# Two layers on one core: reordered scan output, scan-input work moved off GpSimd, attention squares, residual add and prologue moved

## The reference, cut to what matters

```
L0 attention:  h_tan = arcsinh(|h|)/|h| * h ;  q,k,v = h_tan @ w*.T        (16 heads of 16)
               q_hyp, k_hyp = sinh(|.|)/|.| * (.) ;  times = sqrt(1/c + |.|^2)
               probs = softmax(-(q_hyp.k_hyp - q_time*k_time)/4) ;  out = probs @ v @ wo.T
L0 ffn:        fp4 quantised gate/up/down, silu(gate)*up
L1 scan:       x_in, z = split(x @ in_w.T) ;  u = silu(conv4(x_in)) ;  dt, B, C from u
               dt = clip(softplus(dt_raw*w + b), 1e-4, 10)
               h_t = h_{t-1}*exp(dt_t*A) + dt_t*B_t*u_t ;  y_t = h_t.C_t       (512 channels x 16 states)
               out = (layernorm(y)*g + b + D*u) * silu(z) @ out_w.T
L1 ffn:        token-shift mix, sigmoid(r) * (relu(k)^2 @ W_v)
```

## Time and profile before

| phase | us from the start | span, us |
|---|---|---|
| attention | 0 to 2957 | 2957 |
| first ffn | 2957 to 3645 | 688 |
| scan input | 3645 to 4335 | 690 |
| scan | 4335 to 5715 | 1380 |
| scan output | 5715 to 6122 | 407 |
| last ffn | 6122 to 6371 | 249 |
| span of the profiled execution | | 6371.1 |
| profiled execution, device time | | 6372.78 |
| median of three runs | | 6380.58 |

### The profile page before, as it was taken

How to read it: one execution, slowest core, us unless ns; L and a number is a source line. 1 busy time by engine, 2 the same in 40 slices (tenths; PEclk the granted TensorE clock), 3 DMA queues, 4 the chain that set the end, 5 groups by cost and what they waited for, 6 DMA issues and landing times. The chain is left out here.

```text
span 6371.1 us, 94620 instructions
## 1 busy us (share of the span) xinstructions
PE 5160.2 (81%) x27420; PEld 2063.8 (32%) x27420; DVE 4908.5 (77%) x10471; ACT 3773.4 (59%) x5329; POOL 1359.8 (21%) x1658
## 2 busy tenths in 40 slices
PE   6979889797979979796999854426888888877878
PEld 3333333333333333332566522211111111115555
DVE  6666575766667576665888688888999999987768
ACT  4555555555555555553444366666888888874434
POOL 0000000000000000000111134454444444434411
PEclk8989989898989989797999976665555555559999
DMA  0000000000000000000111123332111111124422
GB/s 24 1 14 1 14 1 1 14 1 14 1 14 1 1 14 1 8 1 27 35 41 43 49 88 117 120 117 73 50 49 50 49 50 49 51 68 149 150 91 73
DMA packets 198904, 273.56 MB, mean 43 GB/s; under 512 B 13989, under 2 KB 157989, under 8 KB 192454
## 3 DMA queue, kind: packets, MB, share of 16 engines
q1 hardware_dynamic: 181190, 252.90, 13.0%
q10 hardware_dynamic: 17408, 16.78, 0.8%
HBM read 151.14 MB, written 118.49 MB: 42 GB/s over the span
## 5 line engine op out<-in xcount | busy, mean ns | idle before, releaser
L644 DVE TENSOR_REDUCE at_nmax<-at_ps_t 128x1 f32<-128x512 f32 x2048 | 1320.8, 686 | 583.2 <-PE at_ps_t L344 565.8
L486 ACT ACTIVATE at_probsT<-at_ps_s 128x1024 f32<-128x1024 f32 x1024 | 1045.9, 1023 | 808.8 <-PE at_ps_s L369 808.8
L2044 DVE SCALAR_TENSOR_TENSOR sc_decayed<-sc_da,sc_state 128x256 f32<-128x256 f32 x2048 | 775.5, 424 | 9.3 <-ACT sc_da L1999 8.2
L2054 DVE CUSTOM_DVE_ANT_0 sc_state<-sc_xd,sc_decayed 128x256 f32<-128x256 f32 x2048 | 755.6, 408 | 0.0
L2006 ACT ACTIVATE sc_xd<-sc_ps_du,sc_bt 128x512 f32<-128x512 f32 x1024 | 649.9, 692 | 176.8 <-PE sc_ps_du L1947 176.8
L344 PE MATMUL at_ps_t<-at_qkT 108*128 108x512 bf16 x2048 | 711.0, 412 | 42.9 <-DVE at_nmax L644 19.5
L1912 POOL TENSOR_SCALAR sc_xd<-sc_xd 128x1024 f32<-128x1024 f32 x512 | 532.2, 1039 | 804.9 <-ACT sc_xd L2006 804.9
L1936 PE MATMUL sc_da<-sc_parts,sc_sel 24*128 24x512 bf16 x1024 | 566.0, 609 | 118.5 <-DMA sc_sel<-sc_sel 81.6
L1947 PE MATMUL sc_ps_du<-sc_parts,sc_sel 24*128 24x512 bf16 x1024 | 565.2, 609 | 112.5 <-ACT sc_xd L2006 112.5
L378 PE MATMUL at_ps_o<-at_probsT,at_v 128*32 128x256 f32 x8192 | 632.7, 392 | 1.2
L365 PE MATMUL at_ps_s<-at_qkT 108*128 108x512 bf16 x2048 | 623.6, 387 | 0.0
(11 more groups left out here) (308 smaller groups left out, 7990.8 us busy)
## 6 DMA issues: line engine op xcount, KB each, us to landing
dt_parts<-si_pt SPq DMA_DIRECT2D x64, 384.0 KB, 2.6
du_parts<-si_pu SPq DMA_DIRECT2D x64, 384.0 KB, 3.2
sc_parts<-dt_parts SPq DMA_DIRECT2D x128, 192.0 KB
sc_parts<-du_parts SPq DMA_DIRECT2D x128, 192.0 KB
u_tok<-si_ut SPq DMA_DIRECT2D x8, 2048.0 KB, 8.3
y<-sc_yo SPq DMA_DIRECT2D x256, 64.0 KB
so_yin<-y SPq DMA_DIRECT2D x32, 512.0 KB
so_uin<-u_tok SPq DMA_DIRECT2D x32, 512.0 KB
```

The costliest lines, as they stand in the source:

```text
L486: nc.scalar.activation(probsT[:, c % RING, :], ps_s[c % 2][:], ACT.Exp).then_inc(s_exp, 1)
L644: nc.vector.tensor_reduce(nmax[:, par, c, t:t + 1], ps_t[c][:], AX_X, ALU.max, negate=True).then_inc(s_max, 1)
L2044: nc.vector.scalar_tensor_tensor(decayed[:, ch], da[q % 2][:, j % 2, ch], DECAY_MIN, state[:, (j - 1) % SRING, ch], ALU.max, ALU.mult).the ...
L2054: nc.vector._custom_dve(bass.dve_ops.TENSOR_ADD_SAT, out=state[:, j % SRING, ch], in0=xd[:, q % RING, j % 2, ch], in1=decayed[:, ch], s0=S ...
```

## The change

In attention: `LEAD` 14 to 12; `joined` from tile 2 to 4, `row_turned` and `rows_stored` from tile 5 to 6; POOL's hbo behind the splits of heads 0 and 1; in `finish`, ACT's squares two at a time behind the first four attT copies and the roots behind the fifth, DVE's series behind its fourth residual add and the log arguments behind the seventh.

In scan input: 1+exp on ACT (`raised`), the remainders on DVE (`rests`), POOL left with one memset; the tile buffers four deep; ACT's split in two halves (`first_parts` of tile t, `second_parts` of t-1), DVE's third parts of t-2; the convolution writes u directly instead of acc.

In scan output: the turning of the gated result is put first in PE's step and the gT copies first in ACT's; the store of p-3 and the x root of p-2 stand in step p, `x_norm` is done for p-2; xsum, xout and x statistics get two buffers; SP's loads no longer wait for x_sums (only the residual's load does); the first two steps are written out ahead of the loop.

```diff
-    LEAD = 14
+    LEAD = 12
             def splits(b):
                 split(b, 0, 0)
                 split(b, 1, 1)
+                nc.gpsimd.tensor_tensor(hbo[:], hb[:], bo_bc[:]...broadcast_to([P, TB, D]), ALU.add).then_inc(s_hbo, 1)
...
             def finish(b, more):                                     # ACT
-                if more:
-                    squares(b + 1)
-                    log_roots(b + 1)
                 for t in range(TB):
                     ...
                     nc.scalar.copy(attT[:, u]...)
+                    if more and t < QUAD:
+                        square(2 * t)
+                        square(2 * t + 1)
+                    if more and t == QUAD:
+                        log_roots(b + 1)
...
         def _(pool):                                                 # scan input
             nc.gpsimd.memset(xc[:, :, 0:PAD], 0.0).then_inc(s_zero, 1)
-            with pool.Fori(0, B) as b:
-                for t in range(TB):
-                    nc.gpsimd.tensor_tensor(ex1[:, t], ex[:, t], one_col..., ALU.add).then_inc(s_ex1, 1)
-                for t in range(TB):
-                    nc.gpsimd.tensor_tensor(dt[:, w], dt[:, w], pt[:, w, 0], ALU.subtract).then_inc(s_tr, 1)
-                    nc.gpsimd.tensor_tensor(du[:, w], du[:, w], pu[:, w, 0], ALU.subtract).then_inc(s_ur, 1)
+            def raised(t):                                           # ACT
+                nc.scalar.activation(ex1[:, t], ex[:, t], ACT.Copy, bias=1.0).then_inc(s_ex1, 1)
                 for t in range(TB):                                  # ACT
-                    split(b - 1, t)
+                    first_parts(b - 1, t)
+                    if t >= 1:
+                        second_parts(b - 1, t - 1)
-                for t in range(1, TB):                               # DVE
-                    products(b, t)
-                    third_parts(b, t - 1)
+                for t in range(1, TB + 2):
+                    if t < TB:
+                        products(b, t)
+                    if t <= TB:
+                        rests(b, t - 1)
+                    if t >= 2:
+                        third_parts(b, t - 2)
...
             def step(p, w):                                          # scan output, SP
-                sp.wait_ge(s_sum, p - 2)
                 sp.wait_ge(s_turned, 2 * p - 2)
                 sp.wait_ge(s_cent, 2 * p - 2)
                 sp.wait_ge(s_skip, 2 * p - 2)
                 load(p, w)
+                    sp.wait_ge(s_sum, p - 2)
                 load_residual(p - 1, 1 - w)
             def step(p, w):                                          # PE
+                gated_turned(p - 1, 1 - w)
                 z_products(p)
                 x_turned(p + 1, 1 - w)
-                out_products(p - 1, 1 - w)
+                out_products(p - 1)
             def step(p, w):                                          # ACT
+                outs(p - 1)
                 gates(p, w)
                 xT_stored(p + 1)
-                outs(p - 1)
-                x_root(p - 1)
+                    store(p - 3, 1 - w)
                 y_root(p + 1)
-                store(p - 1)
+                    x_root(p - 2, w)
             def step(p, w):                                          # DVE
                 x_sums(p - 1, 1 - w)
-                x_norm(p - 1)
+                    x_norm(p - 2, w)
```

More of the change, by code:

```diff
@@ L404, in head @@
                         outputs(b, hd, c - 2)
-                    if c == 5 and left:
+                    if c == 6 and left:
                         row_turned(b, hd + 1, 1 - par)
@@ L671, in head @@
                         row_max(b, hd + ahead, (par + ahead) % 2, t)
-                    if c == 2 and left:
+                    if c == 4 and left:
                         joined(b, hd + 1, 1 - par)
@@ L893, in finish @@
                     nc.vector.tensor_tensor(hbo[:, t], ps_o[t % 2][:, 0:D], hbo[:, t], ALU.add).then_inc(s_y, 1)
+                    if more and t == QUAD - 1:
+                        log_series(b + 1)
+                    if more and t == QUAD + 2:
+                        log_arguments(b + 1)
                 dve.wait_ge(s_y, b * TB + TB)
@@ L1448, in ssm_input_phase @@
         s_stu = sem("u_saved")
[L1449 to L1450 removed]
+        s_stt = [sem(f"dt_parts_saved{w}") for w in range(RING)]
+        s_std = [sem(f"du_parts_saved{w}") for w in range(RING)]
         x_v = x2.rearrange("b (n p) d -> p b n d", p=P)
@@ L1668, in _ @@
             for t in range(TB):
-                split(B - 1, t)
+                first_parts(B - 1, t)
+                if t >= 1:
+                    second_parts(B - 1, t - 1)
+            second_parts(B - 1, TB - 1)
         @block.vector
@@ L2128, in ssm_output_phase @@
         s_x3 = sem("x3_ready")
-        s_st = sem("x3_saved")
+        s_st = [sem(f"x3_saved{w}") for w in range(2)]
         tiles = lambda a: a.rearrange("b (n p) d -> p (b n) d", p=P)
@@ L2137, in schedule @@
             first()
-            with eng.Fori(0, PAIRS // 2 - 1) as it:
+            step(1, 1)
+            step(2, 0)
+            with eng.Fori(1, PAIRS // 2 - 1) as it:
                 step(2 * it + 1, 1)
@@ L2164, in step @@
                 load(p, w)
+                if not (isinstance(p, int) and p == 2):
+                    sp.wait_ge(s_sum, p - 2)
                 load_residual(p - 1, 1 - w)
@@ L2169, in _ @@
             load_residual(0, 0)
-            with sp.Fori(0, PAIRS // 2 - 1) as it:
+            step(2, 0)
+            step(3, 1)
+            with sp.Fori(1, PAIRS // 2 - 1) as it:
                 step(2 * it + 2, 0)
@@ L2221, in z_products @@
             def z_products(p):
-                pe.wait_ge(s_zs, 2 * p)
+                if not (isinstance(p, int) and p == 0):
+                    pe.wait_ge(s_zs, 2 * p)
                 for u in range(2):
@@ L2236, in out_products @@
                     last.then_inc(s_gt, 1)
-                pe.wait_ge(s_sum, p)
+            def out_products(p):
+                if not (isinstance(p, int) and p == 0):
+                    pe.wait_ge(s_sum, p)
                 for u in range(2):
@@ L2343, in x_sums @@
                     dve.wait_ge(s_o, 2 * p + u + 1)
-                    last = nc.vector.tensor_tensor(xsum[:, u], ps_o[u][:, 0:D], xres[:, w, u], ALU.add)
+                    last = nc.vector.tensor_tensor(xsum[:, w, u], ps_o[u][:, 0:D], xres[:, w, u], ALU.add)
                 last.then_inc(s_sum, 1)
@@ L2362, in y_gated @@
                 dve.drain()
-                if not (isinstance(p, int) and p == 0):
+                if not (isinstance(p, int) and p < 2):
                     dve.wait_ge(s_gt, 2 * p - 2)
@@ L2393, in step @@
                 x_sums(p - 1, 1 - w)
-                x_norm(p - 1)
+                if not (isinstance(p, int) and p < 2):
+                    x_norm(p - 2, w)
             def last_steps():
                 y_gated(PAIRS - 1, 1)
-                for p, w in ((PAIRS - 2, 0), (PAIRS - 1, 1)):
-                    x_sums(p, w)
-                    x_norm(p)
+                x_sums(PAIRS - 2, 0)
+                x_norm(PAIRS - 3, 1)
+                x_norm(PAIRS - 2, 0)
+                x_sums(PAIRS - 1, 1)
+                x_norm(PAIRS - 1, 1)
             schedule(dve, first, step, last_steps)
```

144 lines of the change are left out of this document (79 added, 65 removed).

## The result

The changed kernel takes 6226.41 us, the median of four runs (6223.75 to 6227.39), against 6379.23 us for the kernel before (6377.47 to 6382.16): a ratio of 0.976, 95% interval 0.974 to 0.978. That is 153 us less. The forecast was 6223. Part of so close a hit is luck: 157 us were forecast, and from one profiled execution to the other (6372.78 and 6226.35 us) 146 were gained; the rest of the 153 is that the profiled execution of the kernel before ran 6 us under its median.

The account below looks back on a forecast made before the run. No engine was full in the three phases: waits bound scan output, and POOL slowed DVE in scan input and at one attention copy. 53 + 46 + 58 = 157 us off 6380.6 gave 6223 us, range 6200 to 6250.

Parts of the forecast that it names:

- the loads were no limit: Scan output, rival (a): loads set the pace at 12 us a pair, gain 12 us instead of 58, 6269 us; chance 0.12.
- the ring of rival (d): Scan output: PE's turning, DVE's product, ACT's silu and z wait on each other, 18.5 us a pair, 6490 us; chance 0.02.
- the 0.2 us for the skip term: Scan output: allowance per pair for POOL's skip term sharing something with DVE, raising DVE's step from 9.7 to 9.9 us.
- convolution: Scan input: DVE's convolution of a batch, with POOL idle and a 0.9 us late token start, falls from 24.4 to 20.2 us.
- wait: Scan input: new DVE wait at the first remainder for ACT's first cast, 2.7 us a batch, lost in full.
- tile: Scan input: a token tile on DVE becomes eight instructions of 0.60 us and one of 0.34, 5.14 us.
- The 1 us a turn kept for the edges: Scan input: 1 us a loop turn deducted for effects of four-deep buffers and the longer ACT queue at the edges.
- advice that the forecast set against the change: Scan input: move work off saturated DVE to Scalar or GpSimd; by it alone the phase sum would be 67 us worse.
- Projection and packing: Attention: DVE's copy no longer blocked by POOL's residual add, 4.3 us in each batch but the first, 30 us.
- Heads: Attention: two tiles moved from the prologue are made up in the main loop on PE, costing 0.9 us a batch.
- Finish: Attention: first attT copy starts 2.6 us sooner, net 1.1 us a batch, 8 us in all, bounds -5 to 18.
- the 1.5 us a batch set aside for squares and roots between the copies: Attention finish: deductions of 0.5 us for squares and about 1.0 us for roots with a table load.

Follow-up runs that it names:

- parts_a: Kernel after with POOL's residual add back in front of the heads, 1+exp back on POOL, scan output's loads behind the sums again; 6260.6 us.
- parts_c: Kernel after with squares and roots before attT copies, DVE's series before its residual adds, remainders one tile later, no bias in skip term (output lacks it); 6186.3 us.
- warm_late: Kernel after with 24 idle identity transposes on PE in front of its wait for DVE at a batch's start in scan input; 6214.1 us.
- parts_b: Kernel after with a prologue of 14 tiles, the two remainders back on POOL, scan output's root, norm and store one pair back; 6283.4 us.
- two: Kernel after with scan output's normalising moved from DVE to ACT and scan input's remainders one tile later; 6191.6 us.

## Why the prediction was right

**What bounds the phases.** In scan output the reading of who sets the pace held: PE's wait for gT went, DVE became the pace, the loads were no limit (parts_a), the ring of rival (d) stayed open (PE waits 1.7 us for the product, and DVE for nothing). Of the sizes, 48 us in each phase against 58, 46 and 53, those of scan input were met term by term, and that of attention is a sum of misses that partly cancel.

**Scan output, 58 against 48.** The term that was mis-sized is the 0.2 us for the skip term. With one of POOL's two operations gone a pair is 0.86 us shorter (9.46 against 10.32, parts_c). The forecast said that the adds "move to another place in the step"; it did not look where. They begin when DVE's product ends, and last some 5.7 us; DVE's next 4 us are statistics and a PSUM add, which ran at their length, and the normalising behind them is caught by the fourth. In the kernel before it mostly was not (453 ns in the mean, 809 now). That is 2 x 0.36 = 0.7 us a pair, 22 us in all; without it a pair would be 9.6 us, close to the 9.7 that the forecast worked out for DVE without contention.

**Scan input, 46 against 48.** Each term was met: convolution 20.3 (20.2 forecast), wait 2.37 (2.7), tile 5.15 (3913.03 to 3918.18; 5.14 forecast). The 1 us a turn kept for the edges was 1.1, but that it fits is luck: its cause was not the buffers or the queue, it is TensorE's clock at the start of a batch (warm_late). The 16 instructions added to DVE cost nothing net, since each had been paid for in slowed neighbours: parts_b gives the same work back to POOL and loses 27 us. What the forecast did not see is that its two moves do not add up: with the remainders on DVE the move of 1+exp brought nothing (parts_a), with them on POOL the kernel before and parts_b differ by 21 us (687.6 and 666.6; parts_b also has the deeper buffers and the split in halves). The Trainium skill's rule on the two sides of SBUF (SBUF — State Buffer, SBUF: two separate sides), that a DVE operation with two SBUF inputs and a GpSimd operation that reads SBUF exclude each other, agrees with these rows. The Trainium skill's advice that the forecast set against the change (Perfetto Trace Analysis, Optimizing Scalar/DVE Operations) goes on to say that moving work between GpSimd and DVE might not help, since they share a read port; the forecast left that out. Here such a move off DVE cost 27 us.

**Attention, 53 against 48.** The parts, from the starts of projection, prologue, first logits and last output of all batches, are these. Projection and packing fell from 81.0 us to 76.8 in batches 1, 3, 5 and 7, by 4.2 us where 4.3 was forecast, but to 78.3 to 78.6 in 2, 4 and 6: 24 us and not 30. Prologue 20.2 to 17.5, 8 x 2.7 = 22 us, as forecast. Heads +1.2 us a batch, 0.9 forecast, but batch 0's +7.0. Finish 19.6 to 17.0, 18 us where 8 was forecast: the 1.5 us a batch set aside for squares and roots between the copies did not show. So 48 came near 53 by misses both ways: the forecast had 14 us too much in the projections and the heads, and 10 too little in the finish.

The two shortfalls, in the projections and in batch 0's heads, are one thing. In batch 2 the eighth projection ran at half clock, in batch 3 it did not, with the same wait in front of it:

```profile
769.15 4.34 PE L434 MATMUL at_ps_s<-at_wqkvT,at_hT 128*128 128x512 f32 x8 [2.23 <-ACT at_hT L581]
```
```profile
1129.91 2.85 PE L434 MATMUL at_ps_s<-at_wqkvT,at_hT 128*128 128x512 f32 x8 [2.24 <-ACT at_hT L581]
```

And batch 0's first 22 us of heads ran at 0.50, in parts_c, whose instructions there are the same, at 0.81. In the windows view, from the first logits to 141.3 us, the kernel after and then parts_c:

```profile
119.25:141.30 22.05, 22.05 (x88) 5.22 (x88) 9.01 (x16) 8.90 (x9) 5.59 (x6) 0.50 0.06 16
```
```profile
118.31:141.30 22.99, 22.90 (x135) 6.50 (x135) 13.96 (x23) 12.43 (x14) 5.62 (x6) 0.81 0.15 46
```

The eight other kernels with this prologue gave 247.0 to 247.3 us for batch 0, and the six with the whole phase unchanged gave 2907.4 to 2911.6 us for attention; so the 48 of the profiled run would be 49 to 53 in them. What decides in which batch the clock is late stays open. With the same code in attention the eighth projection was slow in batches 2, 4 and 6 in the kernel after and in 1, 3, 5 and 7 in two; in the kernel before it never was. The Trainium skill (TensorE: Matmul & The Clock Gate, Part 1: The HAM clock gate (the "warmup" mystery)) says that the activity is sampled by an interval that runs freely and doesn't start with the work, which would make it a matter of chance; no run here shows that.

## What to carry to other kernels

In this kernel a DVE operation on SBUF (with two inputs, and copies and tensor_scalar too) that met a running POOL add got nowhere until the add ended: the 128x2 one ended 0.02 us behind it, the 128x256 normalising 0.15, a 128x512 with two inputs 0.55. Statistics, maxima out of PSUM, reciprocals and adds with an input in PSUM kept their length beside POOL. So lay POOL's work beside those, and give it only what fits there. Work moved off POOL to DVE can be free; price it with the slowing of its neighbours, not with its own length. And price two such moves together, since the second may find nothing left to gain. Where an engine sits on a late result, first ask what stands behind it in its queue: moving the gT copies ahead brought 1.1 us a pair, making the result itself later only 0.4.

## What the hardware showed that was not expected

A 128x2 operation takes 1.07 us beside a POOL add and 0.16 without it. TensorE's clock at a batch's start was worth up to 3.5 us (10.7 us to 7.2 from the arguments to the convolution), and idle transposes that did nothing but run there took 13 us off scan input. And the same instructions in the same order differ by 1.5 us a batch in attention from one batch to the next, at the eighth projection by a granted clock that comes up late.
